# A graph network on one core: ScalarE makes 12 of 31 target one-hot columns in sorting, with comparison numbers in PSUM, and the own one-hots in attention

## The reference

```python
x = _layernorm(x + _L0_gnn_ref(x, edge_attr_128, src, dst, ...))   # sum of edge features per target, MLP
x = _layernorm(x + _L1_gnn_ref(x, edge_index, ...))                # attention
x = _layernorm(x + _L2_gnn_ref(x, edge_index, ...))                # edge MLP, sum per target, node MLP
x = _layernorm(x + _L3_gnn_ref(x, edge_index, ...))                # degree-normalised sum, linear
# layer 0:  agg = segment_sum(edge_attr, receivers)
# layer 1:  score = sum(Q[dst] * K[src]) / sqrt(16), clipped to +-5; attn = softmax over all edges
#           h_out = zeros.at[dst].add(attn * V[src])
```

## Time and profile before

| | |
|---|---|
| median of 3 runs | 5868.11 us (5867.2 to 5871.65) |
| profiled execution, its own time | 5868.77 us |
| its span, first to last instruction | 5866.9 us |
| granted TensorE clock, mean | 0.965 of full speed |
| TensorE busy | 5316.1 us (91%) |
| VectorE busy | 4674.9 us (80%) |
| ScalarE busy | 2572.2 us (44%) |
| GpSimd busy | 2071.5 us (35%) |
| sorting, 100 to 810 us of the span | TensorE 634.4, VectorE 690.9, ScalarE 67.1, GpSimd 324.7 us busy |
| attention, 1082 to 3100 us | TensorE 1968.0, VectorE 1669.2, ScalarE 812.7, GpSimd 703.8 us busy |

### The profile page before, as it was taken

One profiled execution on the slowest core, in us unless ns is written; L12 is line 12 of the kernel. 1 busy time (PEld: TensorE's weight loads), 2 busy tenths in 40 slices (PEclk: granted clock), 3 DMA queues, 4 the chain that ended last, 5 costly groups with the idle time before them and its releaser, 6 DMA issues. The chain is left out here.

```text
span 5866.9 us, 170714 instructions
## 1 busy us (share of the span) xinstructions
PE 5316.1 (91%) x58518; PEld 4689.3 (80%) x58518; DVE 4674.9 (80%) x8022; ACT 2572.2 (44%) x5031; POOL 2071.5 (35%) x1980
## 2 busy tenths in 40 slices
PE   2999989799999999999997779999999997699987
PEld 2888877699999999999995569999999995466645
DVE  6999962588888888888884469999999993488874
ACT  0000024344444344444432347777777762366641
POOL 1444436333333333333332335555555551100000
PEclk9999999999999999999997989999999997899978
DMA  7444421222222222222220123333333330100000
GB/s 114 153 152 152 152 84 68 96 95 92 92 94 90 94 92 92 92 89 97 92 85 17 38 90 130 133 133 131 129 134 131 132 107 17 54 0 1 0 1 24
DMA packets 206213, 523.68 MB, mean 89 GB/s; under 512 B 33555, under 2 KB 85398, under 8 KB 199318
## 3 DMA queue, kind: packets, MB, share of 16 engines
q1 hardware_dynamic: 195936, 518.35, 26.1%
q10 hardware_dynamic: 10179, 4.02, 0.3%
HBM read 485.12 MB, written 37.19 MB: 89 GB/s over the span
## 5 line engine op out<-in xcount | busy, mean ns | idle before, releaser
L1276 PE MATMUL ps<-kv_table,stage 128*128 128x256 bf16 x7644 | 1252.8, 273 | 29.2 <-DVE stage L1132 27.5
L1556 POOL TENSOR_TENSOR parts<-rest 128x512 bf16<-128x512 f32 x624 | 699.4, 1130 | 622.5 <-DVE rest L1609 622.3
L1201 ACT ACTIVATE q_kept<-ps 128x512 f32<-128x512 f32 (+1 forms) x676 | 392.5, 581 | 1157.5 <-PE ps L1279 1157.5
L1746 PE MATMUL ps<-a_table,stage 128*128 128x128 bf16 x7644 | 843.6, 219 | 33.6 <-DVE stage L1585 33.6
L1749 PE MATMUL ps<-window,stage 128*128 128x128 bf16 x7800 | 862.8, 220 | 0.0
L1279 PE MATMUL ps<-window,stage 128*128 128x128 bf16 x7800 | 861.2, 220 | 0.0
L1248 POOL TENSOR_TENSOR message<-message 128x512 f32<-128x512 f32 (+1 forms) x468 | 482.0, 1030 | 986.7 <-ACT message L1210 986.6
L1276 PEld LDWEIGHTS ps<-kv_table,stage 128*128 128x128 bf16 x7644 | 667.6, 98 | 70.7 <-issue 28.1
L1279 PEld LDWEIGHTS ps<-window,stage 128*128 128x128 bf16 x7800 | 654.2, 98 | 59.5
L1140 DVE TENSOR_TENSOR product<-ps,q_kept 128x512 f32<-128x512 f32 (+1 forms) x676 | 451.2, 667 | 300.3 <-ACT message L1203 261.0
L1746 PEld LDWEIGHTS ps<-a_table,stage 128*128 128x128 bf16 x7644 | 534.5, 98 | 34.1 <-issue 34.0
(11 more groups left out here) (350 smaller groups left out, 10473.0 us busy)
## 6 DMA issues: line engine op xcount, KB each, us to landing
stage<-lists SPq DMA_DIRECT2D x312, 768.0 KB, 4.1
edges<-in_edge_attr SPq DMA_DIRECT2D x52, 1984.0 KB, 7.7
stage<-lists SPq DMA_DIRECT2D x104, 896.0 KB, 5.4
window<-qkv_rows SPq DMA_DIRECT2D x52, 288.0 KB, 4.7
qkv_rows<-kv_table SPq DMA_DIRECT2D x26, 384.0 KB, 2.5
window<-ab_rows SPq DMA_DIRECT2D x52, 192.0 KB, 4.4
qkv_rows<-q_parts SPq DMA_DIRECT2D x26, 192.0 KB, 2.0
ab_rows<-a_table SPq DMA_DIRECT2D x26, 192.0 KB, 2.0
```

Source lines behind the costliest of these rows:

```text
L1276: nc.tensor.matmul(kv_ps[n % 2][:, i, :], from_src, kv_table[:, tile, q, :], start=(q == 0), stop=(q == 2))
L1556: pool.tensor_tensor(parts_of(n)[:, 0:nt, D:2 * D], rest[BUFFER[n]][:, 0:nt, :], middle[BUFFER[n]][:, 0:nt, :], ALU.subtract).then_inc(low ...
L1746: nc.tensor.matmul(to[:, i, :], from_src, a_table[:, tile, q, :], start=(q == 0), stop=False)
```

## The change

**In sorting.** Column blocks 19 to 30 of `dst_hot` are made by ScalarE: twelve activations |rel - iota|, one per column block, with `rel`'s column as bias, and then one Relu(1 - that) over all twelve. The step stands behind the list values on ScalarE's queue and ahead of the totals. VectorE makes blocks 0 to 18. The numbers 0..127 and 1..128 are put into PSUM bank 2 once, by two matmuls with the identity, and VectorE's target and bucket one-hots read them there. The totals move from bank 2 to bank 7, so TensorE's totals wait for the turned list to be copied, and the edge sum waits for ScalarE's share as well.

**In attention.** VectorE makes the source one-hot only. ScalarE makes the own one-hot of a unit in two passes over it, behind the exponentials: the absolute difference behind batches 2, 5, 9 and 12, the Relu behind 0, 3, 6 and 10 (units and their order are in the diff). TensorE's first batch of a unit and SyncE's list loads wait for both.

```diff
         moved = sem("moved")
-        TOTALS = ps[0:G, 2, 0:BUCKETS]
+        iota_set = sem("iota_set")
+        IOTA_PS = ps[:, 2, P:2 * P]
+        IOTA1_PS = ps[:, 2, 2 * P:3 * P]
+        TOTALS = ps[0:G, 7, 2 * P:2 * P + BUCKETS]
         PREFIX = ps[:, 3:7, 0:8 * BUCKETS]
...
-        def buckets_dve(dve, hot, ids):
-            return dve.tensor_tensor(hot[:, 0:G, :], over_chunks(iota1[:, 0:BUCKETS], G), over_columns(ids, BUCKETS),
+        def buckets_dve(dve, hot, ids, numbers):
+            return dve.tensor_tensor(hot[:, 0:G, :], over_chunks(numbers[:, 0:BUCKETS], G), over_columns(ids, BUCKETS),
                                      ALU.is_equal)
...
+            SHARE = 19
+            hot_act0 = sem("hot_act0")
+            apart0 = sem("apart0")
             with nc.Block("edge_sums_and_lists") as block:
...
+                    def target_step(j, g, b):
+                        act.wait_ge(summed0, j + 1)
+                        for c in range(SHARE, G):
+                            last = act.activation(dst_hot[b][:, c, :], iota, ACT.Abs, bias=of_group(rel, g)[:, c:c + 1],
+                                                  scale=-1.0)
+                        last.then_inc(apart0, 1)
+                        act.wait_ge(apart0, j + 1)
+                        act.activation(dst_hot[b][:, SHARE:G, :], dst_hot[b][:, SHARE:G, :], ACT.Relu, bias=ones[:, 0:1],
+                                       scale=-1.0).then_inc(hot_act0, 1)
                     def totals_step(j):
...
                         act.activation(vals[0][:, 1, :], of_group(lo1, 0), ACT.Copy).then_inc(vals_kept, 1)
+                        target_step(first * 2, 0, 0)
                         totals_step(first * 2)
                         vals_step(first * 2 + 1, 1, 1)
+                        target_step(first * 2 + 1, 1, 1)
                         totals_step(first * 2 + 1)
...
                                 vals_step(j + 1, g + 1, d)
+                                target_step(j + 1, g + 1, d)
                                 totals_step(j + 1)
...
                     dve.wait_ge(moved0, MOVE + 5)
+                    dve.wait_ge(iota_set, 1)
                     dve.sem_inc(moved, 1)
...
                         dve.wait_ge(paid, j)
-                        buckets_dve(dve, bucket_hot[b], of_group(bucket, g)).then_inc(bucketed, 1)
+                        buckets_dve(dve, bucket_hot[b], of_group(bucket, g), IOTA1_PS).then_inc(bucketed, 1)
...
                         dve.wait_ge(summed0, j + 1)
-                        dve.tensor_tensor(dst_hot[b][:, :, :], over_chunks(iota, G), over_columns(of_group(rel, g), P),
-                                          ALU.is_equal).then_inc(hot0, 1)
+                        dve.tensor_tensor(dst_hot[b][:, 0:SHARE, :], over_chunks(IOTA_PS, SHARE),
+                                          over_columns(of_group(rel, g)[:, 0:SHARE], P), ALU.is_equal).then_inc(hot0, 1)
...
                         dve.wait_ge(paid, first * 2 + 1)
-                        buckets_dve(dve, bucket_hot[0], of_group(bucket, 0)).then_inc(bucketed, 1)
+                        buckets_dve(dve, bucket_hot[0], of_group(bucket, 0), IOTA1_PS).then_inc(bucketed, 1)
                         target_step(first * 2, 0, 0)
...
                     pe.sem_inc(coded, 1)
+                    nc.tensor.matmul(IOTA_PS, ident, iota, start=True, stop=True)
+                    nc.tensor.matmul(IOTA1_PS, ident, iota1[:, :], start=True, stop=True).then_inc(iota_set, 1)
...
                         pe.wait_ge(totals_sb, j + 1)
+                        pe.wait_ge(turned_sb, j)
                         totals_pe(bucket_hot[b]).then_inc(totals_ps, 1)
...
                         pe.wait_ge(hot0, j + 1)
+                        pe.wait_ge(hot_act0, j + 1)
                         pe.wait_ge(added0, j + 1)
...
                     with pe.Fori(0, total, PAIRS) as first:
+                        pe.wait_ge(turned_sb, first * 2 + 1)
                         totals_step(first * 2, 0)
...
                 after(5)
-                buckets_dve(dve, r["hot"], r["bucket"]).then_inc(step, 1)
+                buckets_dve(dve, r["hot"], r["bucket"], iota1[:, :]).then_inc(step, 1)
                 after(9)
...
         hots1 = sem("hots1")
+        own1 = sem("own1")
+        apart1 = sem("apart1")
         slot_hot1 = sem("slot_hot1")
...
                     sp.sem_inc(hots1, 2)
+                    sp.sem_inc(own1, 2)
                     sp.sem_inc(step1, 1)
...
                                 for u in range(4):
+                                    sp.wait_ge(own1, pair * 8 + d * 4 + u + 1)
+                                    sp.sem_inc(sp_waited, 1)
                                     lists_sp(sp, lists_b, lists_in1, pair * 8 + d * 4 + u, g, u, hots1)
...
                         dve.wait_ge(gathered1, pair * NB2 + behind + GATHERED)
-                        dve.tensor_scalar(hots[u % 2][0][:, 0:n], lists_b[u % 2][:, 0, 0:n], lane1[:, :], None, ALU.is_equal)
                         dve.tensor_scalar(hots[u % 2][1][:, 0:n], lists_b[u % 2][:, 1, 0:n], lane1[:, :], None,
...
+                    def own_apart(pair, d, u):
+                        n = (unit_tiles(u)[1] - unit_tiles(u)[0]) * P
+                        behind = d * BATCHES + (UNITS[u - 2][1] if u >= 2 else UNITS[u + 2][1] - BATCHES)
+                        act.wait_ge(lists_in1[u % 2], pair * 64 + d * 32 + u // 2 * 16 + 16)
+                        act.wait_ge(gathered1, pair * NB2 + behind + GATHERED)
+                        act.activation(hots[u % 2][0][:, 0:n], lists_b[u % 2][:, 0, 0:n], ACT.Abs, bias=lane1[:, :],
+                                       scale=-1.0).then_inc(apart1, 1)
+                    def own_hot(pair, d, u):
+                        n, k = (unit_tiles(u)[1] - unit_tiles(u)[0]) * P, pair * 8 + d * 4 + u
+                        act.wait_ge(apart1, k + 1)
+                        act.activation(hots[u % 2][0][:, 0:n], hots[u % 2][0][:, 0:n], ACT.Relu, bias=ones[:, 0:1],
+                                       scale=-1.0).then_inc(own1, 1)
                     def exp(pair, n):
...
                             exp(pair, n)
+                            d, b = n // BATCHES, n % BATCHES
+                            following = (pair, 1) if d == 0 else (pair + 1, 0)
+                            if b in (2, 5):
+                                own_apart(pair, d, b // 3 + 2)
+                            if b in (0, 3, 6):
+                                own_hot(pair, d, b // 3 + 1)
+                            if b in (9, 12) and (d == 0 or ahead):
+                                own_apart(*following, b // 3 - 3)
+                            if b == 10 and (d == 0 or ahead):
+                                own_hot(*following, 0)
                             if n == 1 and behind:
...
                     with act.Fori(0, total, PAIRS) as first:
+                        own_apart(first, 0, 0)
+                        own_hot(first, 0, 0)
+                        own_apart(first, 0, 1)
                         keep(first, 0)
...
                             pe.wait_ge(hots1, pair * 8 + d * 4 + u + 3)
+                            pe.wait_ge(own1, pair * 8 + d * 4 + u + 3)
                         pe.wait_ge(product1, s + 1)
```

## The result

The changed kernel takes 5844.9 us (median of 6 runs, 5837.0 to 5850.5) against 5867.2 (5860.7 to 5871.7): a ratio of 0.9962, with a 95% interval of 0.9949 to 0.9975, or 22 us less. Forecast were 5843 us.

A forecast was written before the change was run, and what follows sets the result against it. VectorE was taken to pace sorting, TensorE close behind, and TensorE to bound attention. Terms -26.7 + 3.4 + 2.7 - 6.3 + 1.7 = -25.2 us took 5868.8 to 5843.6, as median 5843 us; range 5824 to 5864 (its own 5830 to 5857).

The forecast's parts named there:

- Sorting's pace: Sorting steps: relieved VectorE lets TensorE's own order set the pace, 12.84 us instead of 13.39; -26.7 us.
- held rank one-hots: Sorting, VectorE: rank one-hots, reading two SBUF tensors, are held by GpSimd's pay products, 4 us or more; costs nothing.
- First totals late: Sorting's first step: ScalarE's new passes stand ahead of its first totals copy and delay it; +3.4 us.
- Attention, steady: Attention's repeating pairs of groups: VectorE's relief -6.3 us against ScalarE's lateness +2.7 us; other effects zero.
- the fifth wait: Attention, pair boundary: TensorE's 0.25 us wait for GpSimd's message goes with one VectorE one-hot less; -6.3 us over 25.
- lateness behind batch 12: Attention, pair boundary: ScalarE's pass overruns its gap by 0.11 us and delays the next scatter; +2.7 us over 25.
- Attention, start: Attention's start: first own one-hots become two ScalarE passes in a row behind a table load; +1.7 us (0 to 3.2).
- The other stages are untouched: Stages outside sorting and attention: the change does not touch them, so no time was forecast for them.
- A: Rival, sorting and attention: ScalarE's passes are dearer or their delays reach TensorE; 5856 to 5870, take 5862 us; chance 0.15.
- B: Rival, slower, attention: exponentials and absolute values need different activation tables, loads around each pass; about 6675 us; chance 0.07.
- C: Rival, faster, attention: VectorE's relief removes all five TensorE waits of a pair; about 5802 us; chance 0.05.
- D: Rival, sorting: PSUM does not free the port, bucket one-hots stay 3.17 us; forecast's time; 0.73 together with the forecast.

The follow-up runs named there:

- e3: Kernel before plus the whole sorting part of the change, attention as before: 5842.4 us, ratio 0.9964.
- e1: Kernel before plus only sorting's numbers in PSUM; VectorE still makes all 31 target column blocks, attention as before: 5841.2 us, ratio 0.9956.
- e4: Kernel before plus the whole attention part of the change, sorting as before: 5869.4 us, ratio 1.0002.
- e8: e4 with 24 unrelated semaphore increments per engine between attention and the second edge stage: 5865.6 us, ratio 0.9999 to the kernel before.
- e9: Changed kernel with 24 unrelated semaphore increments per engine between attention and the second edge stage: 5849.3 us, ratio 0.9968 to the kernel before.
- e2: Kernel before plus only ScalarE's 12 target column blocks in sorting; numbers stay in SBUF, attention as before: 5846.1 us, ratio 0.9964.
- e7: e3 with the turning matmul moved behind the copied totals and first totals copied before ScalarE's first share: 5805.5 us, ratio 0.9897 to the kernel before.

## Why the prediction was right

The time was met to 2 us, by a sorting term that was right and, for the rest, by luck: attention brought 9 us more than forecast, and 7 us went in stages that the forecast held at nothing, 2 in sorting.

- **Sorting's pace, forecast -26.7 us.** Right in mechanism and size: 13.40 to 12.86 us over 49 steps is -26.4. The 12.84 us of the one step without a wait was what every step became. ScalarE's share took 3.62 + 1.57 = 5.2 us for 5.3 forecast, the held rank one-hots 4.10 us for "4 or more", and neither is on the path.
- **First totals late, +3.4.** The totals are copied at 117.59 for 114.31. Two runs hold it apart from the rest of the start: from the first totals matmul to the first turning matmul are 22.5 us in e3 and 19.0 in e1, a difference of 3.5. The whole start moved only +2.4: from totals to turning it is 20.2 us before and 22.4 in the changed kernel, since the numbers in PSUM alone shorten this stretch by some 1.2 (e1), and the starts of single executions differ by 2 us and more besides (e4 133.8 us, e8 131.6, the same code).
- **Not forecast in sorting: +2.9 us.** The second step is 0.55 us longer (ScalarE's DMA issue took 2.06 us there for 0.32 in the steady step, and with the share behind it the totals come late), and the last is 2.35 longer by the hole and the clock shown above; e9, with a hole of 2.09 us and no fall of the clock, took 11.57 for it, so the clock's part is some 1.6. Sorting in all: -21.1 for -23.3 forecast.
- **Attention, steady: -3.6 forecast (2.7 - 6.3), -12.3 measured** (the stretch's -14.5, of which 2.2 belong to the start, next item). The mis-sized term. The place was right: the fifth wait went. Its price was not the 0.25 us of idle: from scatter to scatter the boundary takes 3.01 us (2379.63 to 2382.64) for 3.42 (2330.02 to 2333.44), and a whole pair 76.91 for 77.38, so 0.47 us x 25 = 12 us. Why a wait of 0.25 us costs 0.41 to 0.47 is not shown. And the +2.7 of lateness behind batch 12 does not show: the next scatter waits 0.18 us, as it did before (0.17).
- **Attention, start: +1.7.** The stretch from the last turning matmul grew by 2.9; from the first gather to the second scatter 11.4 us are left of 13.6, 2.2 less: together +0.7, inside 0 to 3.2. Table load and two passes are in the rows above, in a row as forecast.
- **"The other stages are untouched"** was wrong as a statement on time: +7.2 us from the end of attention on, in unchanged code. This took back more than half of attention's gain, and no term of mine stood for it. The 8.7 us of the second edge stage are mostly the holes shown under e8 and e9 and the lower clock behind them.
- **A slip in the forecast's own range.** The terms named for its upper end (+2.6, +1.5 over the start's 1.7, +13) make 5860, not 5857.

Of the rivals, A (ScalarE takes TensorE's place) shows nowhere: totals and messages do not wait for ScalarE's passes in the steady state. B is refuted by the single table load; the rule of the Trainium skill ("ScalarE: Activation LUTs", "Table sets: the hidden batching unit") that abs and relu are in every set now has a trace beside an exponential. C did not come: four waits stayed, each with its old length. D is refuted by e1 and e2.

## What to carry to other kernels

Where a faster engine feeds the bound one, look for a single step in which it happened to be in time: its pitch is what every step will become, and relief beyond that point buys nothing until the bound engine's own queue is reordered, which here was worth more (0.9964 to 0.9897) than the change itself. Price a removed wait by the pitch between two instructions that repeat, with and without it, not by the idle time shown. And a gain of some 0.1% in one stage can be lost in others whose code did not change, or in the spread of single executions, so time such a part alone before believing its stretch, and compare the granted clock of a stage before comparing its time.

## What the hardware showed that I had not expected

- A wait cost more than its idle time: 0.25 us shown was 0.41 between scatters and 0.47 in the pair. In the sorting step 0.34 us shown went together with 0.75, but there the turning matmul moved too, which is 0.22 of it.
- A hole of 2 to 3 us in TensorE's stream was often followed by some 4 us of lower granted clock (0.58 behind 2.12 us; 0.71 and 0.50 around and behind 3.01 us), but not always: behind the same hole in the last sorting step the clock stayed at 1.00 in e7 (2.06 us) and e9 (2.09 us), and so it did behind 2.85 us in the changed kernel's second edge stage. What decides is open. Behind 0.95 us it stayed at 1.00.
- Single gaps of 0.7 to 5.3 us sit in first and last steps outside a loop, 1.2 to 1.6 us behind the end of an instruction transfer. With 24 unrelated instructions ahead, the one in the second edge stage's first pair vanished and the one in its last pair stayed.
